# Compressed values of an attention as four products of 32 rows side by side, and ten routed batches with their scatters ahead of the last norm

## What is computed

```python
x = _layernorm(x + _L0_attn_ref(x, ...))        # sparse and windowed attention, 16 heads of 128
x = _layernorm(x + _L0_xattn_ref(x, ctx, ...))  # attention to the context
x = _layernorm(x + _L0_ffn_ref(x, ...))
x = _layernorm(x + _L1_attn_ref(x, ...))        # small attention, 32 heads of 8
x = _layernorm(x + _L1_xattn_ref(x, ctx, ...))  # small attention to the context, 16 heads of 16
x = _layernorm(x + _L1_ffn_ref(x, ...))         # 16 experts, the best 6 of each token
```

```python
ctx_sparse = jnp.einsum('bhsk,bhskd->bhsd', pw, v_g)   # v_g: the chosen rows of cv
merged = (ctx_sparse + ctx_local) * 0.5
out = merged... @ Wo + bo
```

## Time and profile before

| | us |
|---|---|
| runs of the kernel before, median (lowest to highest) | 2750.59 (2749.55 to 2751.62) |
| the profiled execution, its own time | 2741.3 |
| its span in the profile | 2739.5 |
| first attention, one tile of the steady part | 49.05 |
| mean granted clock of TensorE | 0.948 |

### The profile page before, as it was taken

One profiled execution on the slowest core, in us unless ns is written; L12 is line 12 of the kernel. 1 busy time (PEld: TensorE's weight loads), 2 busy tenths in 40 slices (PEclk: granted clock), 3 DMA queues, 4 the chain that ended last, 5 costly groups with the idle time before them and its releaser, 6 DMA issues. The chain is left out here.

```text
span 2739.5 us, 50448 instructions
## 1 busy us (share of the span) xinstructions
PE 2321.4 (85%) x16399; PEld 1526.4 (56%) x16545; DVE 1870.4 (68%) x4371; ACT 1589.4 (58%) x3099; POOL 714.6 (26%) x897
## 2 busy tenths in 40 slices
PE   6999999999987567777777689889997986899994
PEld 3676766767664334444444445545555664467773
DVE  5777778777775989999999912256665775234443
ACT  3656666566664679999989911056664654223332
POOL 1121121211210122222222200011111267336664
PEclk9999999999999799999989989999998998899997
DMA  5000000000001599999999920140000022446666
GB/s 199 1 1 0 0 0 0 0 0 0 0 0 47 97 200 189 184 178 188 176 175 191 185 55 1 35 114 1 1 1 7 13 68 79 140 89 109 108 111 142
DMA packets 539447, 211.18 MB, mean 77 GB/s; under 512 B 475002, under 2 KB 533878, under 8 KB 538230
## 3 DMA queue, kind: packets, MB, share of 16 engines
q1 hardware_dynamic: 518246, 180.54, 33.0%
q0 software_dynamic: 20592, 27.98, 5.9%
q10 hardware_dynamic: 416, 0.16, 0.0%
HBM read 54.27 MB, written 36.90 MB: 33 GB/s over the span
## 5 line engine op out<-in xcount | busy, mean ns | idle before, releaser
L1752 DVE TENSOR_SCALAR_CACHE_REDUCE x_row<-x_p_s,x_nsq 128x1024 f32<-128x1024 f32 x512 | 621.6, 1273 | 22.2 <-PE x_p_s L1527 21.8
L1631 ACT ACTIVATE x_ints<-x_row,x_nb 128x2048 uint16<-128x2048 f32 x256 | 511.7, 2000 | 50.9 <-DMA x_turned<-x_ints 32.7
L1527 PE MATMUL x_p_s<-x_kT,x_qz 128*128 128x512 bf16 x929 | 295.2, 406 | 150.2 <-DVE x_row L1752 142.2
L363 POOL TENSOR_TENSOR a_rstd<-a_ssq,neghalf 128x16 f32<-128x16 f32 x32 | 125.9, 3934 | 522.9 <-DVE a_ssq L874 522.9
L1527 PEld LDWEIGHTS x_p_s<-x_kT,x_qz 128*128 128x128 bf16 x1024 | 72.5, 101 | 270.7 <-DVE x_row L1752 246.0
L3276 POOL DMA_INDIRECT f_acc<-f_yt,f_ids x111 | 171.8, 1548 | 135.5 <-ACT f_yt L3441 117.4
L1655 POOL TENSOR_SCALAR x_nb<-x_low,x_hmin 128x1 f32<-128x1 f32 x256 | 74.4, 291 | 505.6 <-DVE x_row L1752 504.3
L1561 PEld LDWEIGHTS x_p_o<-x_vi,x_turned 128*128 128x128 f16 x4096 | 142.8, 97 | 87.1 <-DMA x_turned<-x_ints 19.3
L2215 ACT COPY s_eT<-sc_p_e 128x512 f32<-128x512 f32 x192 | 112.1, 584 | 133.9 <-PE sc_p_e L2105 133.8
L1561 PE MATMUL x_p_o<-x_vi,x_turned 128*128 128x16 bf16 x4096 | 142.3, 170 | 18.6 <-DMA x_turned<-x_ints 18.3
L2105 PE MATMUL sc_p_e<-ident,s_e 128*128 128x128 f32 x768 | 123.7, 285 | 33.0 <-ACT s_eT L2215 21.6
(11 more groups left out here) (479 smaller groups left out, 5314.5 us busy)
## 6 DMA issues: line engine op xcount, KB each, us to landing
f_rows<-f_spread SPq DMA_DIRECT2D x111, 136.5 KB, 2.1
f_w<-in_L_ffn_w_dram SPq DMA_DIRECT2D x2, 2816.0 KB
x_turned<-x_ints SPq DMA_TRANSPOSE x224, 4.8
f_sum<-f_acc SPq DMA_DIRECT2D x6, 512.0 KB, 7.6
f_w<-in_L_ffn_w_dram SPq DMA_DIRECT2D x2, 1408.0 KB
f_spread<-f_empty SPq DMA_DIRECT2D x17, 136.5 KB, 2.5
x_res<-in_x_dram SPq DMA_DIRECT2D x2, 1024.0 KB, 6.9
a_wq<-in_L_attn_Wq_dram SPq DMA_DIRECT2D x2, 1024.0 KB, 10.6
```

What stands on the lines that cost most here:

```text
L363: pool.tensor_tensor(rstd[:, hs], ssq[:, hs], core.neghalf[:, 0:NH], ALU.pow).then_inc(root_h.sem, 1)
L1527: mm = pe.matmul(p_s[n % SLOTS][:, c * BANK:(c + 1) * BANK], qz[b % 2][:, par, a, :], kT[:, a, at:at + BANK], start=True, stop=True)
L1631: act.activation(ints[k][:, :], rows[k][:, :, :].rearrange("p s n -> p (s n)"), ACT.Exp, bias=nb[:, k:k + 1], scale=-1.0, accum_out=esum[: ...
L1752: dve.tensor_scalar(rows[k][:, half, :], p_s[n % SLOTS][:, :], nsq[:, b % 2, h:h + 1], HIGHEST, ALU.mult, ALU.min, accum_out=(low if half ...
```

## The change

Three things are changed.

- **A, first attention.** `cv` is one 128 x 128 tile: the 32 compressed values stand four times below each other. A new piece `sparse_values` makes four products of 32 rows by 512 columns: `cv[rows_of g]` with `psT[rows_of g]`, each into a bank of its own, `context = (p_cT, p_pT, work[0], work[1])`. A group of rows is now one group of values, which the order of heads in the compressed scores provides (`qT` is read in a row, and the scales are broadcast in another shape). `values` adds the 16 products of `raw[2]` to these banks. Since `work[0]` and `work[1]` hold the scores, `sparse_values` waits for all exponentials of its tile (`l_exp.of(b)`); `turn_p0`, `turn_p2` and the first two turns of q wait for the banks to be read. PE's and ACT's orders are rewritten; those of DVE and POOL stay.
- **B, small attentions.** Ten batches, not 11, are routed early, in spans of 4, 4 and 2. POOL's list has up to seven scatters in a step, numbered through over all batches: two in the first step, six in the next four, seven in the next four, six in the last; none comes after the last norm_root. Two batches are staged in a step until all are.
- **C, routed feed-forward.** Six batches, not five, are routed late: 36 scatters, paced by four to a step of PE, not three. Their staged rows lie in tiles that exist already.

```diff
@@ -214,7 +214,7 @@
-        cv = sb("a0_cv", [P, G, D])
+        cv = sb("a0_cv", [P, D])
@@ -253,6 +253,7 @@
+        context = (p_cT, p_pT, work[0], work[1])
@@ -335,7 +336,6 @@
-            pool.memset(cv[:, :, :], 0.0).then_inc(cleared, 1)
@@ -485,7 +485,7 @@
-                        pe.wait_ge(l_exp.sem, l_exp.of(b - 1, NG - 1 + n))
+                        pe.wait_ge(cT_read.sem, cT_read.of(b - 1, NG - 1 + n))
@@ -498,7 +498,7 @@
-                                   qT[:, j::G, :], start=True, stop=True)
+                                   qT[:, j * NG:(j + 1) * NG, :], start=True, stop=True)
@@ -539,23 +539,32 @@
+                    if g in (0, 2):
+                        pe.wait_ge(cT_read.sem, cT_read.of(b, g))
...
+            def sparse_values(b):
...
+                pe.wait_ge(proj_read.sem, proj_read.of(b))
+                pe.wait_ge(c_read.sem, c_read.of(b))
+                pe.wait_ge(cT_read.sem, cT_read.of(b, 0))
+                pe.wait_ge(pT_read.sem, pT_read.of(b, 2))
+                pe.wait_ge(l_exp.sem, l_exp.of(b))
+                for g in range(NG):
+                    rows_of = slice(g * NC, (g + 1) * NC)
+                    pe.matmul(context[g][:, :], cv[rows_of, :], psT[rows_of, :, :].rearrange("p j t -> p (j t)"), start=True, stop=False)
...
-                    pe.wait_ge(cT_read.sem, cT_read.of(b, g))
-                    if g == 0:
-                        pe.wait_ge(proj_read.sem, proj_read.of(b))
-                        pe.wait_ge(c_read.sem, c_read.of(b))
...
-                        o = p_cT[:, h * P:(h + 1) * P]
...
-                        pe.matmul(o, raw[2][:, at:at + D], pT[g % 2][:, h, :], start=(h == 0), stop=False)
-                        mm = pe.matmul(o, cv[:, h, :], psT[:, g, :], start=False, stop=(h == G - 1))
+                        mm = pe.matmul(context[g][:, h * P:(h + 1) * P], raw[2][:, at:at + D], pT[g % 2][:, h, :],
+                                       start=False, stop=(h == G - 1))
@@ -573,7 +582,7 @@
-                      "sparse": sparse_scores, "sparse_back": sparse_back, "turn_sparse": turn_sparse}
+                      "sparse": sparse_scores, "sparse_back": sparse_back, "turn_sparse": turn_sparse, "sparse_values": sparse_values}
@@ -581,9 +590,9 @@
-                     ("s3", 1), ("turn_sparse", 1), ("k2", 0), ("values0", 1), ("turn_p1", 1), ("k3", 0), ("turn_p2", 1),
-                     ("entries", 0), ("values1", 1), ("out0", 1), ("values2", 1), ("turn_p3", 1), ("out1", 1),
-                     ("values3", 1), ("comp_kv", 0), ("v0", 0), ("v1", 0), ("v2", 0), ("v3", 0), ("out2", 1),
+                     ("s3", 1), ("turn_sparse", 1), ("k2", 0), ("turn_p1", 1), ("k3", 0), ("sparse_values", 1), ("values0", 1),
+                     ("values1", 1), ("entries", 0), ("out0", 1), ("turn_p2", 1), ("out1", 1), ("turn_p3", 1), ("values2", 1),
+                     ("comp_kv", 0), ("values3", 1), ("v0", 0), ("v1", 0), ("v2", 0), ("v3", 0), ("out2", 1),
@@ -656,12 +665,7 @@
-                if isinstance(b, int) and b == 0:
-                    act.wait_ge(cleared, 1)
-                for h in range(G):
-                    q = slice(NC * h, NC * (h + 1))
-                    last = act.copy(cv[q, h, :], bank[q, D:2 * D])
-                last.then_inc(proj_read.sem, 1)
+                act.copy(cv[:, :], bank[:, D:2 * D]).then_inc(proj_read.sem, 1)
@@ -723,7 +727,7 @@
-                    act.copy(cT[g % 2][:, :, :].rearrange("p g t -> p (g t)"), p_cT[:, :]).then_inc(cT_read.sem, 1)
+                    act.copy(cT[g % 2][:, :, :].rearrange("p g t -> p (g t)"), context[g][:, :]).then_inc(cT_read.sem, 1)
@@ -736,9 +740,9 @@
-                      ("square_q", 0), ("turn_sparse", 1), ("exp2", 1), ("turn_p1", 1), ("values0", 1), ("exp3", 1),
-                      ("turn_p2", 1), ("values1", 1), ("values2", 1), ("turn_p3", 1), ("entries", 0), ("square_k", 0),
-                      ("comp_kv", 0), ("v0", 0), ("v1", 0), ("v2", 0), ("v3", 0), ("values3", 1)], pieces, B, before=1)
+                      ("square_q", 0), ("turn_sparse", 1), ("exp2", 1), ("turn_p1", 1), ("exp3", 1), ("values0", 1),
+                      ("values1", 1), ("entries", 0), ("turn_p2", 1), ("turn_p3", 1), ("values2", 1), ("square_k", 0),
+                      ("comp_kv", 0), ("v0", 0), ("v1", 0), ("values3", 1), ("v2", 0), ("v3", 0)], pieces, B, before=1)
@@ -951,7 +955,9 @@
-                dve.tensor_tensor(scm[:, :, :], scm[:, :, :], bcast(rqs[:, :], [P, NH, NC]), ALU.mult).then_inc(s_arg.sem, 1)
+                placed = scm[:, :, :].rearrange("p (m g) c -> p m g c", g=NG)
+                scales = rqs[:, :].rearrange("p (g m) -> p m g", m=G).unsqueeze(3).to_broadcast([P, G, NG, NC])
+                dve.tensor_tensor(placed, placed, scales, ALU.mult).then_inc(s_arg.sem, 1)
@@ -1816,8 +1822,8 @@
-    "pool": [("spread1", 1), ("scatter2", 9), ("scatter3", 9), ("residual", 0), ("root_qk", 0), ("scatter4", 9), ("scatter5", 9),
-            ("spread0", 0), ("norm_root", 3), ("scatter0", 8), ("scatter1", 8)],
+    "pool": [("spread1", 1), ("scatter0", 8), ("scatter1", 8), ("residual", 0), ("root_qk", 0), ("scatter2", 8), ("scatter3", 8),
+            ("spread0", 0), ("scatter4", 8), ("norm_root", 3), ("scatter5", 8), ("scatter6", 8)],
@@ -2357,7 +2363,7 @@
-SPANS, REST = ((0, 4), (4, 4), (8, 3)), (11, 5)
+SPANS, REST, LEFT = ((0, 4), (4, 4), (8, 2)), (10, 6), 2
@@ -2516,7 +2522,7 @@
-        self.batches, self.looked = REST[0], REST[0] + 1
+        self.batches, self.looked = REST[0], REST[0] + LEFT
@@ -2575,15 +2581,15 @@
-                dst = s.raw[:, b - SPANS[n][0], :] if b < s.batches else s.weights.left[:, 0, :]
+                dst = s.raw[:, b - SPANS[n][0], :] if b < s.batches else s.weights.left[:, b - s.batches, :]
...
-        def stage(b):
-            if b < s.batches:
+        def stage(step):
+            for b in [lo + j for lo, m in SPANS for j in range(m) if lo + j // 2 == step]:
@@ -2631,9 +2637,18 @@
-        def scatter(k):
-            def run(b):
-                if b < s.batches:
+        waiting = [(b, k) for b in range(s.batches) for k in range(CHOICES)]
+        planned, filled = {}, 0
+        for step in range(B):
+            for place in range(CHOICES + 1):
+                if (step > 0 or place > 4) and (step > 4 or place != 4) and filled < len(waiting):
+                    planned[step, place] = waiting[filled]
+                    filled += 1
...
+        def scatter(place):
+            def run(step):
+                if (step, place) in planned:
+                    b, k = planned[step, place]
@@ -2642,7 +2657,7 @@
-        return {f"scatter{k}": scatter(k) for k in range(CHOICES)}
+        return {f"scatter{place}": scatter(place) for place in range(CHOICES + 1)}
@@ -3115,7 +3130,7 @@
-        self.base, self.left = sb("base", [P, B + 1, EXPERTS]), sb("left", [P, 1, EXPERTS])
+        self.base, self.left = sb("base", [P, B + 1, EXPERTS]), sb("left", [P, LEFT, EXPERTS])
@@ -3166,7 +3181,6 @@
-        staged = [sb(f"staged{i}", [P, WIDE]) for i in range(LATE)]
@@ -3179,6 +3193,7 @@
+        staged = [sums[1][i // 3][:, :, :].rearrange("p g h -> p (g h)")[:, i % 3 * WIDE:(i % 3 + 1) * WIDE] for i in range(LATE)]
@@ -3206,7 +3221,7 @@
-            return 1 + m // 3
+            return 1 + m // 4
@@ -3512,8 +3527,8 @@
-            dve.tensor_copy(raw[:, 0:1, :], weights.left[:, :, :]).then_inc(raw_up, 1)
-            dve.tensor_copy(raw[:, 1:, :], p_x[0][:, 0:GROUP * EXPERTS].rearrange("p (g e) -> p g e", e=EXPERTS)).then_inc(raw_up, 1)
+            dve.tensor_copy(raw[:, 0:LEFT, :], weights.left[:, :, :]).then_inc(raw_up, 1)
+            dve.tensor_copy(raw[:, LEFT:, :], p_x[0][:, 0:GROUP * EXPERTS].rearrange("p (g e) -> p g e", e=EXPERTS)).then_inc(raw_up, 1)
```

## The result

The changed kernel takes 2837.51 us (median of two executions) and the kernel before 2750.59; the ratio is 1.0298, 95% interval [1.0262, 1.0333]. It is slower: by 82 us going by the ratio, by 87 going by the two medians, and not by the 39 of the forecast. The profiled execution of after took 2836.51, span 2834.7. One execution among all that follow is a disturbed one, the profiled one of `fx_three` (4868 us, where its six others took 2728 to 2741); it stands in no ratio.

The account below looks back on a forecast made before the run. The first attention was taken as bound by PE. To the profiled 2741.3 us came +30 (longer tiles), +0.8 (last tile), +17 (clock) and -9 (part B): +39, 2780, or 2789 as a median; range 2742 to 2814.

Parts of the forecast that it names:

- The new wait: First attention: PE stalls 3.25 us a tile ahead of the products of 32 rows, until all four exponentials end.
- The late chain square_k, sum_k, root_k, comp_norm: First attention: square_k behind values2's late copy moves the chain 2.99 us later; PE waits another 1.2 ahead of comp_key.
- the rival in which root_k falls to 2.91: First attention: POOL's root_k takes 2.91 us, not 4.97, and the clock stays; period +0.8, total 2755; chance 0.10.
- The period without a clock fall: First attention: the tile's period grows by 2.0 us from 49.05, to some 51 where the clock stays.
- Part A's saving: First attention, PE: sixteen products of cv, 3.57 us, replaced by four side by side, 1.14; gain 2.43 us a tile.
- Part B behind the norm: End of the small attentions: with no scatter after the last norm_root, the last POOL work ends 9.5 us earlier.
- I count half of the tiles: 1.15 x 15 = +17: First attention: slow clock after the stall costs 2.3 us in half of the tiles; +17 us, ends 0 and +35.
- part C at nothing: Routed stage: six more late scatters, 7.6 us, lie beside PE's work, covered by 17 us before the first loads; zero.
- Its upper end of +8: Routed stage: part C costs up to 8 us if the late scatters lack cover before the loads that read them.
- +48 for part A: First attention: +30 for 15 longer tiles, +0.8 for the last tile, +17 for the slow clock.
- -9 for B and C: Small attentions and routed stage: B nets -9 us after dearer scatter steps, ends -4 and -12; C counts zero.
- clock falls in every tile: First attention: the granted clock drops after the stall in every tile, 17 us above the forecast, 2806; chance 0.13.

Follow-up runs that it names:

- fx_three: The order of fx for part A plus parts B and C, late scatters three to an expert step instead of four: 2731.87 us, ratio 0.9923 to the kernel before.
- a_fill: Kernel before plus part A alone, with three unread 128x512 products in PE's wait ahead of the products of 32 rows: 2807.88 us.
- a_fillsq: Kernel before plus part A alone, with three unread filling products in PE's wait and ACT's square_k moved ahead of turn_p2: 2769.07 us.
- fx: Kernel before plus part A alone, reordered: next-tile work under PE's wait, DVE's next k2 ahead of prob2, square_k ahead of turn_p2: 2742.92 us, ratio 0.9961.
- a_square: Kernel before plus part A alone, with ACT's square_k moved ahead of turn_p2: 2808.58 us.
- bc_late: Kernel before plus parts B and C alone, the 36 late scatters four to a step but held back by three expert steps: 2753.33 us, ratio 0.9994.

## Why the prediction was wrong

**Right by its own steps.** The new wait: 3.04 for 3.25, at the place and for the reason given. The late chain square_k, sum_k, root_k, comp_norm makes PE wait 0.99 for 1.2; the rival in which root_k falls to 2.91 is out (4.97). The Trainium skill's page "SBUF — State Buffer", "SBUF: two separate sides", says that a DVE operation with two SBUF inputs and a GpSimd operation lock each other out for a whole instruction. The 5.1 that the forecast estimated by it is near the measured 4.97. The period without a clock fall: 51.24 for 51.1. In that agreement two errors meet: the wait for the exponentials is 0.2 shorter than forecast, and the late chain costs 1.7 a tile and not 1.2, as a_fill and a_fillsq show. Part A's saving: 3.57 - 1.07 = 2.50 for 2.43, so the four products do run side by side. The Trainium skill's page "TensorEngine Tiling (Array Packing)", "Key Properties", says that a change of mode drains TensorE. The rows show little that this could be: in fx the first piece of values behind the products takes 1.00 to the next start (474.03 to 475.03), the second 0.89 (to 475.92), so some 0.1. Part B behind the norm: 8.4 for 9.5.

**Wrong: the clock.** The step that failed is "I count half of the tiles: 1.15 x 15 = +17". The argument was that the stage is dense on both sides of the gap, like the place in the earlier trace rows where the clock stayed. It fell in 13 of 14 periods, and a fall of the steady part costs 3.4 (3.1 against the tile of a_fill) and not 2.3: 40 us in these fourteen. The upper end was too low as well: its +35 took 2.3 for every tile, although the 3.2 was in the text as the upper price, and 3.4 is above that too. a_fill shows the term: the same wait for the exponentials, PE kept busy in it, clock 1.00, 51.52 a tile. The rows had said it: five of seven gaps were followed by a slow stretch, 6 us long behind the very row that was shown; a gap that comes back in every pass of a loop deserved at least that share. The Trainium skill's page "TensorE: Matmul & The Clock Gate", section "HAM oscillation — how this bites in real kernels", describes a loop of this kind: every pass waits, there for a DMA, and the next one starts slow. The trace agrees, 13 of 14.

**Wrong: part C at nothing.** "Beside PE's work, covered by 17" asked only whether the scatters end in time. They do (24.5 us before f_rows). The cost is on the other side: they delay the work they stand beside, the shared expert: from f_sum to the last f_acc store 93 and 98 us at four to a step, where it was 80 to 87. Its upper end of +8 was for lost cover, a thing that did not happen.

**The sum.** +48 for part A became 77, -9 for B and C became +5; 82 in all, and 2837.51 lies outside the range of 2742 to 2814. In the profile the first attention is 80.5 longer: 23 of the 33 us beyond the forecast are the clock's (40 for 17), and 9 lie ahead of the first period and behind the last (2.0 and 7.9, where the forecast had 0.8 for the last tile). The rival "clock falls in every tile", 2806, was the right mechanism, given 0.13, at too low a price.

## What to carry to other kernels

A wait put into a dense PE loop is paid twice: its length, and the slow clock behind it in each pass, here 3.04 and 3.4 us; price the second at every pass unless rows of such a loop say otherwise (here it came in 13 of 14), and look first for work of the next pass to put under the wait (fx turned +5.6 a tile into -1.3). When DMAs are moved "beside" other work, ask not only whether they end in time but what they do to that work, and leave room in their pace. A saving is worth taking apart even when the change loses: here both parts pay, once one order and one number are mended.

## What was not expected of the hardware

- A stall of 3.04 us is followed by 6.8 us at 0.50 in the last nine tiles of after and by 3.4 in most of a_square; the shorter stretch is met in after too (52.67, 53.15), the longer one in a_square (52.80), and once, in the tile of 51.24, none at all.
- A wait costs more than its idle time: PE's last piece ahead of the 3.04 takes 1.88 where 1.72 is its pitch (566.03 to 567.75 for the piece of keys before it), and comp_key behind the 0.99 takes 0.33 where the earlier trace rows have 0.27.
- Beside scatters issued by POOL, ACT and DVE start 3.4 to 6 us after the product of PE that they need has ended (bc_late), for which the profile names no cause; in before, with 30 scatters there, PE's groups follow 1.16 us apart.
